# A routed expert stage on one core: down weights loaded as 112 and 4 partitions, and the weighted down product first in VectorE's step

## What is computed

```python
topk_idx = jax.lax.top_k(scores_for_choice, K)[1]          # 6 of 128 experts for each token
buf_idx = jnp.where(pos < CAP, se * CAP + pos, E * CAP)    # 192 places for each expert
xb = x[token_buf].reshape(E, CAP, H)                       # gather: 128 x 192 x 192
gu = jnp.einsum('ech,ehf->ecf', xb, W_gate_up)             # 192 -> 2 x 464
g, u = jnp.split(gu, 2, axis=-1)
inter = jax.nn.silu(g) * u
yb = jnp.einsum('eci,eih->ech', inter, W_down)             # 464 -> 192
yb = yb * w_buf.reshape(E, CAP, 1)                         # weight of each token at this expert
routed = jnp.zeros((T, H), x.dtype).at[token_buf].add(yb.reshape(E * CAP, H))
```

## Time and profile before

| | |
|---|---|
| median of the runs | 4345.16 us |
| span of the profiled execution, first to last instruction | 4339.1 us |
| PE busy | 3835.0 us, 88% |
| DVE busy | 3261.9 us, 75% |
| ACT busy | 2637.8 us, 61% |
| POOL busy | 3020.4 us, 70% |
| moved by DMA | 473.54 MB, mean 109 GB/s |

### The profile page before, as it was taken

The page is one execution under the profiler, slowest core; times in us unless marked ns, Lnnn a source line. Parts: engine busy times, 40 slices in busy tenths (PEclk is TensorE's granted clock), DMA queues, the critical chain, the costliest instruction groups (busy, mean ns, idle before and its releaser), DMA issues. The chain is left out here.

```text
span 4339.1 us, 74496 instructions
## 1 busy us (share of the span) xinstructions
PE 3835.0 (88%) x22114; PEld 2899.2 (67%) x22114; DVE 3261.9 (75%) x5523; ACT 2637.8 (61%) x4838; POOL 3020.4 (70%) x1609
## 2 busy tenths in 40 slices
PE   3469999999999999999999999988879999999997
PEld 2346666666676666766666666656558888888886
DVE  1788888888889888898888988887246666666663
ACT  1468877888778888788887788875522222222221
POOL 0888888878788787887888878886025555555554
PEclk8669999999999999999999999999989999999999
DMA  3333333333333333333333333321057777777775
GB/s 81 86 85 82 93 90 91 99 83 89 94 84 92 92 84 94 88 94 96 82 90 94 92 89 92 89 71 53 16 127 183 186 184 185 184 183 185 184 186 115
DMA packets 243533, 473.54 MB, mean 109 GB/s; under 512 B 39644, under 2 KB 162080, under 8 KB 243220
## 3 DMA queue, kind: packets, MB, share of 16 engines
q1 hardware_dynamic: 203792, 429.90, 37.4%
q0 software_dynamic: 36864, 37.98, 5.6%
q10 hardware_dynamic: 2564, 1.82, 0.2%
HBM read 404.99 MB, written 64.56 MB: 108 GB/s over the span
## 5 line engine op out<-in xcount | busy, mean ns | idle before, releaser
L507 POOL TENSOR_TENSOR y<-y,state 128x972 f32<-128x972 f32 x448 | 1016.8, 2270 | 336.0 <-DVE state L668 325.3
L486 POOL TENSOR_TENSOR state<-du,b_rows 128x972 f32<-128x972 f32 x512 | 1187.7, 2333 | 3.0
L662 DVE TENSOR_TENSOR_SCAN ps<-ps,state 128x972 f32<-128x972 f32 x512 | 1113.6, 2181 | 61.1 <-ACT ps L530 47.6
L530 ACT ACTIVATE ps<-delta,a_neg 128x324 f32<-128x324 f32 x1536 | 727.3, 521 | 313.0 <-DVE state L668 250.8
L1040 POOL DMA_INDIRECT out_rows<-yo,scatter_idx x256 | 369.5, 1443 | 426.9 <-DMA out_rows<-yo,scatter_idx 354.0
L668 DVE TENSOR_TENSOR state<-ps,c_rows 128x972 f32<-128x972 f32 x512 | 597.7, 1168 | 35.2 <-DVE ps L662 0.5
L782 PE MATMUL ps<-ws_d,inter 116*98 116x192 f32 (+1 forms) x3072 | 539.2, 329 | 16.3 <-issue 12.9
L782 PEld LDWEIGHTS ps<-ws_d,inter 116*98 116x98 f32 (+1 forms) x3072 | 501.7, 175 | 24.2 <-issue 16.3
L1171 PE MATMUL e_ps<-w_down,e_inter 116*96 116x192 f32 x2048 | 359.9, 329 | 102.1 <-DVE yo L1121 102.1
L754 DVE TENSOR_TENSOR inter<-ag,ps 116x648 f32<-116x648 f32 x256 | 211.5, 826 | 316.9 <-PE ps L767 316.9
L1102 DVE TENSOR_TENSOR e_inter<-e_ag,e_ps 116x384 f32<-116x384 f32 x256 | 139.9, 555 | 375.1 <-ACT e_ag L1066 366.6
(11 more groups left out here) (174 smaller groups left out, 7333.4 us busy)
## 6 DMA issues: line engine op xcount, KB each, us to landing
b_rows<-bc_rows SPq DMA_DIRECT2D x256, 324.0 KB, 5.0
c_rows<-bc_rows SPq DMA_DIRECT2D x256, 324.0 KB, 5.7
w_lo<-in_we_up SPq DMA_DIRECT2D x128, 348.0 KB
w_down<-in_we_down SPq DMA_DIRECT2D x128, 348.0 KB
x_in<-in_x SPq DMA_DIRECT2D x32, 1176.0 KB, 7.7
w_hi<-in_we_up SPq DMA_DIRECT2D x256, 116.0 KB
image_cnt<-running_counts SPq DMA_DIRECT2D x256, 81.0 KB
w_lo<-in_we_up SPq DMA_DIRECT2D x128, 116.0 KB
```

The source lines that it names most:

```text
L486: nc.gpsimd.tensor_tensor(b.state[n % 4][:], b.du[t.p][:], row, ALU.mult).then_inc(input_ready, 1)
L507: nc.gpsimd.tensor_tensor(y, y, b.state[n % 4][:], ALU.add).then_inc(y_added, 1)
L530: ins = nc.scalar.activation(to[:, c * L:c * L + L], b.delta[t.p][:, c, :], ACT.Exp, scale=b.a_neg[:, c, k:k + 1])
L662: nc.vector.tensor_tensor_scan(s, s, b.state[k % 4][:].rearrange("p a t -> p (a t)"), 0.0, ALU.mult, ALU.add).then_inc(scan_done, 1)
```

## The change

One transfer becomes two, and one part changes its place in DVE's list. `EVEN` is 112, the largest multiple of 16 in the 116 partitions. The down weights are loaded as partitions 0 to 111 and partitions 112 to 115; both transfers count on the same semaphore, so PE waits for 32 per use of the buffer in place of 16. DVE does `("down", 2)` first in its step and not fourth.

```diff
+EVEN = HC // 16 * 16
...
-    "dve": (("up", 0, 0), ("up", 0, 1), ("weigh", 0), ("down", 2), ("token", -5), ("one_hot", -6), ("dot", -1)),
+    "dve": (("down", 2), ("up", 0, 0), ("up", 0, 1), ("weigh", 0), ("token", -5), ("one_hot", -6), ("dot", -1)),
...
-                        sp.dma_start(w_down[t.q][:], a["we_down"][bass.ds(t.v, 1)].rearrange("o p c f -> p (o c) f")).then_inc(down_loaded[t.q], 16)
+                        down = a["we_down"][bass.ds(t.v, 1)].rearrange("o p c f -> p (o c) f")
+                        sp.dma_start(w_down[t.q][0:EVEN], down[0:EVEN]).then_inc(down_loaded[t.q], 16)
+                        sp.dma_start(w_down[t.q][EVEN:HC], down[EVEN:HC]).then_inc(down_loaded[t.q], 16)
...
-                        pe.wait_ge(down_loaded[t.q], 16 * t.h + 16)
+                        pe.wait_ge(down_loaded[t.q], 32 * t.h + 32)
```

## The result

The changed kernel takes 4208.24 us (median of four runs, 4202.63 to 4215.05), the kernel before beside it 4344.62. The ratio is 0.9689 with a 95% interval of 0.9678 to 0.9700: 136.4 us less, where 129.8 were forecast.

What follows compares the result with a forecast made beforehand. PE bound the expert stage, waiting each step for DVE's `yo`, beside an equally long scatter cycle. Gains of 119.8, 6.0 and 4.0 us (pipeline end) made 129.8: span 4209.3, plus 6.1 to the median, 4215.4 us; range 4207 to 4250.

Steps and rivals of the forecast that it cites:

- What bounds the stage: Expert stage: PE bounds it, busy 91%, in a rigid cycle with 102.1 us idle before the down product, awaiting DVE's `yo`.
- 119.8 + 6.0: Expert stage: 121 steps at 0.99 us give 119.8 us; steps 123 to 126 at 1.5 us each give 6.0.
- the price of the wait: PE's wait for `yo` costs 0.99 us per step, 8.71 against 7.72 in the step without it.
- 6.1 us from span to median: Whole kernel: the median time was taken as 6.1 us above the profiled span.
- The reorder and its condition: DVE: moving `yo` first removes PE's wait, 0.99 us a step, if the scatter has freed its buffer in time.
- The limit of 4.5 us for a landing: POOL: PE reaches 7.72 us steps only if scatters land within 4.5 us of their second issue, after 3.21 of issue.
- The split: Down-weight load: 112 partitions spread over sixteen engines in place of four, adding no bytes; costs SP one issue, 0.26 us.
- The landing: POOL's scatters: with the load spread they land in 3.0 us in place of 5.50, a cycle of 6.2 us.
- The second: Rival: the down-weight load doesn't spread, DVE waits for `added`, only the end gains; 4341 us, 25 either way; chance 0.05.
- the scatter cycle of 8.71 us: POOL: 3.21 us of issue and 5.50 of landing, as long as PE's step; assumed to stay if the load doesn't spread.
- the third rival: Slower: DVE's `yo` waits for scatters with `inter` behind it, landing over 5.50 us; 4405 us at 6.0; chance 0.04.
- The first rival: Landings improve too little, 4.5 to 5.5 us; at 5.0 the step is 8.21 us, time 4279 us; chance 0.08.

Runs made afterwards that it cites:

- the run with more bytes: The changed kernel, also loading the 112 partitions of down weights a second time per expert into unread buffers; 4214.35 us against 4340.84 for the kernel before.
- four buffers: Kernel before with only DVE's `yo` moved first, plus four buffers each for `yo` and row numbers in place of two; 4382.56 us against 4340.38.

## Why the prediction was right

**What bounds the stage.** Right. The two stages can be set side by side by their first waiting step and the last expert's up product; of before, two starts in order of time (the first in the earlier trace rows, at 3221.68), and of after:

```profile
4310.55 0.49 PE L1157 MATMUL e_ps<-xgt,w_lo 128*116 128x192 f32 x2
```

```profile
3225.54 0.49 PE L1160 MATMUL e_ps<-xgt,w_lo 128*116 128x192 f32 x2
...
4188.57 0.49 PE L1160 MATMUL e_ps<-xgt,w_lo 128*116 128x192 f32 x2
```

1088.87 us became 963.03: 125.8 less, where 119.8 + 6.0 were forecast. From there to the end of the span 28.6 us became 24.5: 4.1, where 4.0 were forecast. Reading the price of the wait off the one step without it (0.99 us) and not off the idle time (0.80 in the mean) was worth 24 us in the sum. The profiled spans differ by 126.0 and not by 129.9 because this execution entered the stage 3.9 us later, which no part of the change touches. The median gained 136.4, 6.6 more than forecast, and lies only 1.2 us above the lower end of the range; the kernel before alone had medians from 4340.4 to 4344.6 in these runs, so the rest is not to be explained from one profile. One term of the sum was too large: 6.1 us from span to median. Each execution's time lies only some 2 us above its span (4215.05 against 4213.1 in the profiled one); the other 4 were the profiled execution of before, faster than its median. That 4215.4 was forecast and 4215.05 measured for the profiled execution is therefore luck in part: those 4 us and the late entry into the stage cancel.

**The reorder and its condition.** Right in both: `yo` was finished 2.6 us before PE needed it, and alone the reorder made DVE wait behind `added`. The limit of 4.5 us for a landing fits the run with more bytes, which stayed just inside it in the mean and kept PE full.

**The split.** Right that the load would spread: 112 partitions ran on sixteen engines (a share of 0.95), where 116 ran on four. Of the two rules of the Trainium skill (DMA: Bandwidth & Descriptors), the one on divisors ("Why a DMA increments its semaphore by 16 and not by 1") agrees with that. The one against two transfers ("Rules for kernel authors") gives as its reason that both halves run on all sixteen engines either way; 116 partitions ran on four, so it doesn't hold for this load, and the measurement decides. The landing was mis-sized a little: 3.0 us was taken because twelve engines carried the scatter undisturbed, and the semaphore events give 3.35 in the mean. POOL's own rows give more, since they show only landings that it waited for. The only one under load took 3.97, from the end of the first row's issue to the second's start:

```profile
4164.07 1.44 POOL L1043 DMA_INDIRECT out_rows<-yo,scatter_idx  x1 [0.30 <-issue]
...
4169.48 1.45 POOL L1043 DMA_INDIRECT out_rows<-yo,scatter_idx  x1 [1.08 <-DMA out_rows<-yo,scatter_idx]
```

The margin to 4.5 was 1.15 us in the mean, where the prediction had 1.5, and it was enough. With PE full at its full clock, none of the runs points to a version that beats the changed kernel.

**The rivals.** The second, a split that doesn't spread, came out as a run: the reorder alone. It was priced at 4341 with 25 us either way and measured at 4374.75. The step that failed was taking the scatter cycle of 8.71 us over unchanged. With the reorder alone the landing grew from 5.5 to 5.8 us in the mean, with some of 6 to 8; that the regular step of the kernel before had kept it short is likely, but not shown. So the reorder without the split belongs to the third rival, slower through landings over 5.50, though not by the mechanism given there: four buffers took DVE's wait away and not the loss. The first rival, a stage between, came true only for the split of 76 and 40, and there with two paces and not with one longer step.

## What to carry to other kernels

What the removal of a wait is worth can be read off a step that hasn't got it; here the trace had such a step at the start of the pipeline. Before an instruction is moved ahead, look for the cycle that runs beside the one being shortened, since it becomes the pace; here two edits, each worthless or harmful alone, were worth 3% together. A transfer can load few engines by its number of partitions alone (116 ran on four here, 112 on sixteen), and the price appears elsewhere: at another queue's transfers, here the scatters, and at the queue that issued it.

## What the runs showed of the hardware

Counted from the end of its second issue to POOL's next one, a scatter landed in 2.66 us with no loads, in 3.35 in the mean with the 348 KB of down weights on sixteen engines, in 4.0 with 336 KB more on sixteen, and in 5.5 with the 348 KB on four. On two engines, the issuing queue itself was held for 4.58 us by one instruction that otherwise took 0.26. And on sixteen engines, 253 GB/s with a DMA share of 1.03 left PE full, so a mean share near one is no proof of a bound.
